# Attention steps reordered on every engine of a cross-attention and mixture-of-experts kernel, with TensorE's steps written out

## The chip, the cores and the metric

The kernel runs on one core of a Trainium2 chip. The metric is device time in microseconds of one execution. An engine issues its own instructions in program order, and engines meet only at semaphores. PE is TensorE, DVE is VectorE, ACT is ScalarE, POOL is GpSimd, and SP issues most of the DMAs.

## The reference

The input is 4 x 512 rows of 512 numbers. One layer of cross-attention (8 heads of 64 channels) and one mixture-of-experts layer with a shared expert follow each other, both with a residual.

```python
def _L0_xattn_ref(q, k, v, gamma):
    qk = jnp.einsum('bhdq,bhdl->bhql', qh, kh) * scale
    sm = jax.nn.softmax(qk, axis=-1)
    ret = jnp.einsum('bhql,bhdl->bhdq', sm, vh)
    return gamma * ret.reshape(B, Dv, Lq)
def _L0_ffn_ref(hidden_states, router_w, w_gate, w_up, w_down, sw_gate, sw_up, sw_down, shared_gate_w):
    shared = jnp.einsum('ts,sh->th', jax.nn.silu(x @ sw_gate) * (x @ sw_up), sw_down)
    ...
    routed = jnp.einsum('eth,te->th', expert_out, combine)
    shared_out = jax.nn.sigmoid(x @ shared_gate_w)[:, None] * shared
    return (routed + shared_out).reshape(B, S, Hd)
x = x + _L0_xattn_ref(_layernorm(x), ctx_2048, ctx_2048, L0_xattn_gamma)
x = x + _L0_ffn_ref(_layernorm(x), ...)
```

Queries are the normalised `x`; keys and values are both the context. Heads run over the channel rows, so 128 rows of `x` hold two heads.

## The kernel before

The kernel has three stages on the time axis: attention (to about 260 us), the shared expert (lines with `wsp`), and the routed experts. Only the first stage and what it hands over are touched. Every fp32 product is made of a rounded high half and the low rest (`qh`, `ql`, `kh`, `kl`, `pth`, `ptl` and so on).

Attention works on NT = 16 tiles of 128 rows, which is two heads each. For a tile `t` the work is, with the letters that the text uses:

- SP: `load_x` and `load_values` bring `xb` and `cn`; `store_rows`, `store_normed` and `store_columns` write the results.
- DVE `first_norm`, `aggregate(0)`, `variance(0)`, then POOL `inverse_deviation(0)`, `shift(0)`, `queries`, `queries_hi`, `queries_lo`, `keys_hi`, `keys_lo`: the operands of the scores.
- S0 to S3 (`scores`): six matmuls each on PE, into one of two double PSUM tiles. After each, DVE takes the maximum (`maxima`, L919) and ACT two exponentials (`exps`, L677). S(c+2) reuses the PSUM tile of S(c).
- T0 to T7 (`probs_T`, L1226): four transposes each on PE into one of the three PSUM banks `bT`, by the table `P_BANK`. ACT copies the high half (`probs_hi`, L683), DVE takes the rest (`probs_lo`, L929), and only then is the bank free. T0 to T3 want the exponentials of the first head, of which S3's is last.
- V0 to V7 (`times_v`, L1240 and L1242): two matmuls each into `bO`. After V3 and V7 ACT copies one half of the result (`low_half`, L696) and DVE adds (`halves`, L936), which frees `bO`.
- Val (`values_T`, L1254), Inv (`inverses`, L1248), Row (`rows_T`, L1260) and Log (`logits`, L1266) on PE: context transpose, softmax divisors (spread by POOL's `spread`), transposed rows of the result, and router logits.
- POOL `scaled`, `residual`, then DVE `second_norm`, `aggregate(1)`, `variance(1)`, then POOL `inverse_deviation(1)`, `shift(1)`, `rows_normed`: the rows `x2n` that Row transposes.

A step `i` mixes parts of tiles `i-4` to `i+4`. Each engine has its own list in a function `step(i)`, and that list is the only thing that sets the order. On PE step `i` of before holds T4 to T7 and V2 to V7 of tile i-1, S3 and T0 to T3 of tile i, and S0 to S2 of tile i+1. On PE steps 4 to 13 are five turns of a hardware loop with two steps in each turn, and waits whose values come from registers; all other steps and all other engines are written out.

In steps 9 to 12 POOL's list ends with `first_tokens`, which splits 128 tokens of the shared expert's first block (L568, L571). In step 16 ACT and DVE split the first two chunks of the shared expert's weights (`weights_hi`, `weights_lo`, 128 x 1536). PE begins the shared expert with `gate_up(0, 0)` and `gate_up(0, 1)`, which stand between the last attention steps; its first `down` is at L1366.

At the start SP's list runs `load_x(0)`, `load_values(0)`, `load_x(1)`, `load_values(1)`, `load_x(2)`, `small_ones()`, `load_x(3)`. The last line of `small_ones` writes `slot_rows` from `meta`: 39 KB in 4992 pieces of 8 bytes.

## Time and profile before

| | us |
|---|---|
| median of 3 runs | 898.32 (897.53 to 900.61) |
| profiled execution | 897.0 |
| its span | 895.2 |
| PE busy in the span | 850.4 |
| DVE, ACT, POOL busy | 568.3, 504.7, 438.6 |

The profile is of one execution: it has a span, and 1.8 us lie around it. Its busy times are of all three stages together. For the first stage the engines must be read window by window: the whole span has PE at 95%, but DVE at 63% only because the two later stages leave it idle, and the page's 40 slices show DVE at nine tenths through most of the first ten.

### The profile page before, as it was taken

How to read it: one execution, taken by the hardware profiler on the slowest of the kernel's cores; microseconds unless marked ns; L12 is line 12 of the kernel's file. 1: busy time of each engine (PE TensorE's matmuls, PEld its weight loads, DVE VectorE, ACT ScalarE, POOL GpSimd, SP SyncE). 2: the span in 40 equal slices, each digit the busy share in tenths (PEclk: the TensorE clock that was granted, in tenths of full speed). 3: DMA queues.
4: the chain of work that ended last, by engine and by line, in shares of the span. 5: the costliest groups of instructions: out<-in, count | busy, mean ns of one | idle time of the engine just before them, and what ended most of it. 6: DMA issues, size and time to landing. Idle time of an engine off the chain costs nothing.

```text
span 895.2 us, 13754 instructions
## 1 busy us (share of the span) xinstructions
PE 850.4 (95%) x4624; PEld 709.4 (79%) x4624; DVE 568.3 (63%) x819; ACT 504.7 (56%) x862; POOL 438.6 (49%) x422
## 2 busy tenths in 40 slices
PE   4999999999869999999999999999999999999993
PEld 2677777777658888888888888888899999999992
DVE  4999999999625533421312121125899999999991
ACT  4999999889543321121112111114888888888881
POOL 6576777875500000043320000002799999999983
PEclk9999999999979999999999999999999999999996
DMA  9113232241343313000310015444844444344342
GB/s 119 61 72 107 94 140 98 81 152 60 118 141 106 106 48 128 13 2 2 122 23 24 1 69 184 158 168 164 257 78 88 72 81 83 70 84 81 71 71 35
DMA packets 63236, 81.24 MB, mean 91 GB/s; under 512 B 15369, under 2 KB 34825, under 8 KB 63186
## 3 DMA queue, kind: packets, MB, share of 16 engines
q1 hardware_dynamic: 53426, 60.14, 22.0%
q0 software_dynamic: 9760, 20.49, 12.7%
q8 instruction: 25, 0.41, 0.2%
q14 instruction: 25, 0.20, 0.1%
HBM read 53.01 MB, written 27.60 MB: 90 GB/s over the span
## 4 chain that ended last, share of the span: by engine, by line
PE 86%; POOL 5%; DVE 3%; issue 2%; ACT 2%; DMA 2%; POOLq 0%; SPq 0%; DVEq 0%; ACTq 0%
PE scores L1352 9%; PE scores L1353 9%; PE scores L1354 9%; PE bank L1226 5%; PE scores L1217 5%; PE bank L1366 5%; PE bank L1367 5%; PE bank L1368 5%; PE bank L1453 3%; PE bank L1454 3%; PE bank L1452 3%; PE bank L1240 3%; PE scores L1428 3%; PE scores L1430 3%; PE scores L1429 3%; PE bank L1428 3%
## 5 line engine op out<-in xcount | busy, mean ns | idle before, releaser
L1009 DVE TENSOR_TENSOR sg<-scores,sg 128x512 f32<-128x512 f32 x44 | 30.4, 692 | 216.0 <-PE scores L1354 201.8
L1352 PE MATMUL scores<-x_hl,wsp 128*128 128x512 f32 x352 | 137.1, 389 | 0.0
L1354 PE MATMUL scores<-x_hl,wsp 128*128 128x512 f32 x352 | 137.0, 389 | 0.0
L1353 PE MATMUL scores<-x_hl,wsp 128*128 128x512 f32 x352 | 137.0, 389 | 0.0
L608 POOL DMA_INDIRECT slot_rows<-msrc,posi x32 | 33.4, 1045 | 185.4 <-PE scores L1354 178.9
L623 POOL DMA_INDIRECT xg<-x_normed_rows,meta x39 | 40.1, 1029 | 160.5 <-PE scores L1376 141.8
L782 ACT ACTIVATE sg<-scores 128x512 f32<-128x512 f32 x44 | 26.3, 598 | 159.7 <-PE scores L1354 159.7
L677 ACT ACTIVATE pb<-scores,negmax 128x512 f32<-128x512 f32 x128 | 88.1, 695 | 12.2 <-DVE negmax L919 12.2
L789 ACT ACTIVATE hh<-sg 128x512 fp32r<-128x512 f32 x44 | 27.8, 631 | 115.9 <-DVE sg L1009 100.9
L929 DVE TENSOR_TENSOR ptl<-bank,pth 128x512 fp32r<-128x512 f32 x128 | 87.1, 683 | 6.1 <-ACT pth L683 5.6
L919 DVE TENSOR_REDUCE negmax<-scores 128x2 f32<-128x1024 f32 x64 | 77.8, 1215 | 9.3 <-PE scores L1217 8.7
L683 ACT ACTIVATE pth<-bank 128x512 fp32r<-128x512 f32 x128 | 76.7, 600 | 12.1 <-PE bank L1226 10.9
L644 POOL TENSOR_TENSOR wd<-wex,wd 96x512 fp32r<-96x512 f32 x39 | 80.5, 2065 | 3.3
L1226 PE MATMUL bank<-ident,pb 128*128 128x128 f32 x512 | 78.6, 276 | 1.6 <-DVE ptl L929 1.5
L1226 PEld LDWEIGHTS bank<-ident,pb 128*128 128x128 f32 x512 | 60.1, 140 | 25.1 <-issue 9.8
L1366 PE MATMUL bank<-wsp,hh 128*128 128x512 f32 x176 | 69.8, 396 | 7.8 <-DVE hl L1011 7.2
L1352 PEld LDWEIGHTS scores<-x_hl,wsp 128*128 128x128 f32 x352 | 66.2, 188 | 13.8
L1353 PEld LDWEIGHTS scores<-x_hl,wsp 128*128 128x128 f32 x352 | 66.1, 188 | 13.7
L1354 PEld LDWEIGHTS scores<-x_hl,wsp 128*128 128x128 f32 x352 | 66.1, 188 | 13.7
L1125 DVE TENSOR_TENSOR wg<-wex,wg 128x1408 fp32r<-128x1408 f32 x39 | 63.4, 1627 | 12.5 <-ACT wg L808 12.5
L634 POOL DMA_INDIRECT out<-y,meta x39 | 63.7, 1634 | 13.0 <-issue 5.8
L1367 PE MATMUL bank<-wsp,hh 128*128 128x512 f32 x176 | 69.4, 394 | 0.0
(175 smaller groups left out, 2224.4 us busy)
## 6 DMA issues: line engine op xcount, KB each, us to landing
wex<-in_L_ffn_w_gate SPq DMA_DIRECT2D x8, 704.0 KB, 4.5
wex<-in_L_ffn_w_up SPq DMA_DIRECT2D x8, 704.0 KB, 5.9
xb<-in_x SPq DMA_DIRECT2D x16, 256.0 KB, 2.8
cn<-in_ctx SPq DMA_DIRECT2D x16, 256.0 KB, 2.7
x_rows<-xb SPq DMA_DIRECT2D x16, 256.0 KB, 2.0
x_normed_rows<-x2n SPq DMA_DIRECT2D x16, 256.0 KB, 2.0
x_normed_transposed<-x2T SPq DMA_DIRECT2D x16, 256.0 KB, 2.0
x_hl<-x_normed_transposed SPq DMA_DIRECT2D x4, 1024.0 KB, 5.2
```

The costliest lines, as they stand in the source:

```text
L634: g.indirect_dma_start(out=out, out_offset=bass.IndirectOffsetOnAxis(ap=meta[:, s, 0:1], axis=0), in_=y3[s % 2][:, :], in_offset=None, com ...
L644: gp.tensor_tensor(wd3[0:IR, 1, c], wex[0:IR, e, 2 * W3 + (IC - 1) * H:EW], wd3[0:IR, 0, c].bitcast(F32), ALU.subtract).then_inc(g_wd, 1)
L677: sc.activation(pb[t % 2][s][:, c, :], bSS[c % 2][:, s, :], ACT.Exp, bias=negmax[:, c, s:s + 1], scale=1.0, accum_out=rsum[:, c, s:s + 1]) ...
L683: sc.activation(pth[n % 4][:, :], bT[P_BANK[n]][:, :], ACT.Copy).then_inc(a_pth, 1)
L919: ve.tensor_reduce(negmax[:, c, :], bSS[c % 2][:, :, :], AX_X, ALU.max, negate=True).then_inc(d_max, 1)
L929: ve.tensor_tensor(ptl[n % 4][:, :], bT[P_BANK[n]][:, :], pth[n % 4][:, :].bitcast(F32), ALU.subtract).then_inc(d_ptl, 1)
L1226: ins = te.transpose(bT[P_BANK[n]][:, q * P:(q + 1) * P], pb[par][s][:, q, c * P:(c + 1) * P], ident[:, :])
L1352: te.matmul(bk[:, :], hi, xhi, start=(h == 0), stop=False)
L1353: te.matmul(bk[:, :], hi, xlo, start=False, stop=False)
L1354: ins = te.matmul(bk[:, :], lo, xhi, start=False, stop=(h == HC - 1))
L1366: te.matmul(bY[tt][:, :], th, hi, start=(c == 0), stop=False)
L1367: te.matmul(bY[tt][:, :], th, lo, start=False, stop=False)
```

## The change

Each engine's `step(i)` gets another list; the functions called are the same, apart from the PSUM bank of Inv and Row (from `bT[1]` to `bT[2]`) and the table `P_BANK`. Steps now run from -2 to 19 instead of -4 to 18. PE's loop is gone: its steps are all written out. PE's step `i` now holds T3 to T7 and all V of tile i-1, S2, S3 and T0 to T2 of tile i, and S0 and S1 of tile i+1. POOL does `queries`, `queries_hi`, `queries_lo` and `keys_hi` of tile i+2 in step i, and `keys_lo` a step later. `scaled` and `residual` of a tile come one step later; `first_tokens` moves to steps 10 to 13.

```diff
-        P_BANK = (0, 1, 0, 2, 0, 2, 0, 2)
+        P_BANK = (1, 0, 1, 0, 2, 0, 1, 0)
...
-            for i in range(-4, NT + 3):
+            for i in range(-2, NT + 4):
                 step(i)
...
             def step(i):
+                if there(i - 4):
+                    store_rows(i - 4)
+                    store_columns(i - 4)
+                if there(i + 2):
+                    load_x(i + 2)
+                    load_values(i + 2)
                 if there(i - 3):
                     store_normed(i - 3)
-                if there(i + 2):
-                    load_values(i + 2)
-                if there(i - 3):
-                    store_columns(i - 3)
-                if there(i + 4):
-                    load_x(i + 4)
-                if there(i - 1):
-                    store_rows(i - 1)
...
             load_values(1)
-            load_x(2)
             small_ones()
-            load_x(3)
-            for i in range(NT + 3):
+            for i in range(NT + 4):
                 step(i)
...
+                if there(i - 3):
+                    shift(1, i - 3)
+                if there(i - 2):
+                    scaled(i - 2)
                 if there(i - 3):
                     rows_normed(i - 3)
+                if there(i - 2):
+                    residual(i - 2)
                 if there(i + 1):
-                    queries_lo(i + 1)
                     keys_lo(i + 1)
+                if there(i + 2):
+                    inverse_deviation(0, i + 2)
+                    shift(0, i + 2)
+                    keys_hi(i + 2)
+                    queries(i + 2)
+                if there(i):
+                    spread(i)
+                if there(i + 2):
+                    queries_hi(i + 2)
                 if there(i - 2):
                     inverse_deviation(1, i - 2)
...
+                if there(i + 2):
+                    queries_lo(i + 2)
+                if 10 <= i < 10 + TB:
+                    first_tokens(i - 10)
...
-            for i in range(-4, 4):
-                step(i, i // 2, i % 2)
-            with pe.Fori(2, NI - 1) as half:
-                for par in range(2):
-                    step(2 * half + par, half, par)
-            for i in range(NT - 2, NT + 1):
+            for i in range(-2, NT + 1):
                 step(i, i // 2, i % 2)
             gate_up(0, 0, 0)
             step(NT + 1, (NT + 1) // 2, (NT + 1) % 2)
             gate_up(0, 1, 0)
-            for i in range(NT + 2, NT + 3):
+            for i in range(NT + 2, NT + 4):
                 step(i, i // 2, i % 2)
```

First place: SP's queue at the very start, from the third tile's load in before to the first load of the steps. Before:

```order
L339 DMA xb2_83<-in_x 128x512
L377 DMA gam_53<-in_L0_xattn_gamma 128x1
L378 DMA rg_80<-in_L0_ffn_router_w 8x512
L379 DMA rg_80<-in_L0_ffn_shared_gate_w 1x512
L381 DMA out<-zrow_112 128x512
L382 DMA x2_normed_rows<-zrow_112 128x512
L384 DMA slot_rows<-meta_60 128x39x2
L339 DMA xb3_84<-in_x 128x512
L344 DMA cn0_69<-in_ctx_2048 128x512
```

After:

```order
L377 DMA gam_53<-in_L0_xattn_gamma 128x1
L378 DMA rg_80<-in_L0_ffn_router_w 8x512
L379 DMA rg_80<-in_L0_ffn_shared_gate_w 1x512
L381 DMA out<-zrow_112 128x512
L382 DMA x2_normed_rows<-zrow_112 128x512
L384 DMA slot_rows<-meta_60 128x39x2
L339 DMA xb2_83<-in_x 128x512
L344 DMA cn0_69<-in_ctx_2048 128x512
```

The load of tile 2 (`xb2`) moved from ahead of the small transfers to behind `slot_rows`, into the place that tile 3's load had.

Second place: DVE's queue at the start, from the maximum of S0 of tile 0. `BN_STATS` on `xb2` is `first_norm(2)`. Before:

```order
L919 TENSOR_REDUCE negmax_66<-scores0 128x2
L892 BN_STATS stats_61<-xb2_83 128x6
L919 TENSOR_REDUCE negmax_66<-scores1 128x2
L940 COPY rgT_52<-bank4 128x36
L913 TENSOR_TENSOR vs0_89<-bank6,vs0_89 128x4x128
L919 TENSOR_REDUCE negmax_66<-scores0 128x2
L919 TENSOR_REDUCE negmax_66<-scores1 128x2
```

After:

```order
L915 TENSOR_REDUCE negmax_66<-scores0 128x2
L915 TENSOR_REDUCE negmax_66<-scores1 128x2
L915 TENSOR_REDUCE negmax_66<-scores0 128x2
L888 BN_STATS stats_61<-xb2_83 128x6
L936 COPY rgT_52<-bank4 128x36
L909 TENSOR_TENSOR vs0_89<-bank6,vs0_89 128x4x128
L915 TENSOR_REDUCE negmax_66<-scores1 128x2
```

`first_norm(2)` moved from behind the first maximum to between the third and the fourth; the fourth maximum now stands behind it.

Third place: PE in step 3, around S3 of tile 3 (`scores1`) and Row of tile 0 (`x2n0`). Before:

```order
L1248 MATMUL bank6<-ident_49,rspr_106 128x128 x4
L1240 MATMUL bank4<-pth3_98,vs0_89 128x512
L1242 MATMUL bank4<-ptl3_102,vs0_89 128x512
L1226 MATMUL bank7<-ident_49,pb01_92 128x128 x4
L1217 MATMUL scores1<-kh1_72,qh1_76 128x512 x2
L1217 MATMUL scores1<-kl1_74,qh1_76 128x512 x2
L1217 MATMUL scores1<-kh1_72,ql1_78 128x512 x2
L1226 MATMUL bank5<-ident_49,pb01_92 128x128 x4
L1260 MATMUL bank6<-ident_49,x2n0_108 128x128 x4
L1240 MATMUL bank4<-pth0_95,vs0_89 128x512
L1242 MATMUL bank4<-ptl0_99,vs0_89 128x512
L1226 MATMUL bank7<-ident_49,pb01_92 128x128 x4
```

After:

```order
L1237 MATMUL bank4<-pth2_97,vs0_89 128x512
L1239 MATMUL bank4<-ptl2_101,vs0_89 128x512
L1214 MATMUL scores1<-kh1_72,qh1_76 128x512 x2
L1214 MATMUL scores1<-kl1_74,qh1_76 128x512 x2
L1214 MATMUL scores1<-kh1_72,ql1_78 128x512 x2
L1237 MATMUL bank4<-pth3_98,vs0_89 128x512
L1239 MATMUL bank4<-ptl3_102,vs0_89 128x512
L1223 MATMUL bank6<-ident_49,pb01_92 128x128 x4
L1257 MATMUL bank7<-ident_49,x2n0_108 128x128 x4
L1223 MATMUL bank5<-ident_49,pb01_92 128x128 x4
L1214 MATMUL scores0<-kh0_71,qh0_75 128x512 x2
L1214 MATMUL scores0<-kl0_73,qh0_75 128x512 x2
```

V3 moved from ahead of S3 to behind it, T5 to ahead of it, and T7 and S0 of the next tile now follow Row directly, with V4 and V5 behind.

## Rows read from the trace of the kernel before

**Rows 1.** Busy time by engine, clock and DMA share in one step's window each.
```profile
core 0: us, PE busy (x) PEld busy (x) DVE busy (x) ACT busy (x) POOL busy (x), PEclk, DMA share, GB/s
80.25:93.87 13.62, 13.62 (x94) 10.25 (x92) 13.08 (x23) 12.75 (x31) 9.83 (x14) 1.00 0.29 97
...
148.34:162.62 14.28, 13.71 (x94) 10.25 (x93) 13.14 (x23) 12.75 (x31) 11.64 (x16) 1.00 0.27 93
...
205.47:219.09 13.62, 13.62 (x94) 10.24 (x93) 12.53 (x20) 12.74 (x31) 7.92 (x9) 1.00 0.18 68
```
**Rows 2.** Timeline of PE inside step 6: start, duration, instruction.
```profile
94.78 0.60 PE L1226 MATMUL bank<-ident,pb 128*128 128x128 f32 x4
95.31 0.50 PE L1217 MATMUL scores<-kh,qh 64*128 64x512 f32 x2
...
96.20 0.66 PE L1226 MATMUL bank<-ident,pb 128*128 128x128 f32 x4
96.69 0.60 PE L1260 MATMUL bank<-ident,x2n 128*128 128x128 f32 x4
97.05 0.49 PE L1240 MATMUL bank<-pth,vs 128*128 128x512 f32 x1
...
97.60 0.60 PE L1226 MATMUL bank<-ident,pb 128*128 128x128 f32 x4
97.96 0.48 PE L1240 MATMUL bank<-pth,vs 128*128 128x512 f32 x1
...
98.60 0.50 PE L1217 MATMUL scores<-kh,qh 64*128 64x512 f32 x2
...
101.40 0.96 PE L1266 MATMUL bank<-rgT,x2T 128*128 128x9 f32 x8
102.29 0.50 PE L1217 MATMUL scores<-kh,qh 64*128 64x512 f32 x2
```
**Rows 3.** Timeline of ACT in the same step.
```profile
95.22 0.60 ACT L696 ACTIVATE lob<-bank 64x512 f32<-64x512 f32 x1
...
98.24 0.60 ACT L683 ACTIVATE pth<-bank 128x512 fp32r<-128x512 f32 x1
98.73 0.68 ACT L677 ACTIVATE pb<-scores,negmax 128x512 f32<-128x512 f32 x1
...
99.39 0.60 ACT L702 ACTIVATE x2T<-bank 128x512 f32<-128x512 f32 x1
99.87 0.70 ACT L677 ACTIVATE pb<-scores,negmax 128x512 f32<-128x512 f32 x1
```
**Rows 4.** SP's DMA queue at the start, timeline.
```profile
5.19 0.49 SPq L384 DMA_DIRECT2D slot_rows<-meta  x1
5.72 8.50 SPq L339 DMA_DIRECT2D xb<-in_x  x1
```
**Rows 5.** The tile view of `xb` from 4 to 9 us, which holds that one load.
```profile
DMA to landing us min/median/max: 15.4/15.4/15.4
```
**Rows 6.** Timeline of DVE and of PE: the fourth maximum, and S2 of two tiles.
```profile
17.75 1.23 DVE L919 TENSOR_REDUCE negmax<-scores 128x2 f32<-128x1024 f32 x1 [0.57 <-PE scores L1217]
...
23.99 0.50 PE L1217 MATMUL scores<-kh,qh 64*128 64x512 f32 x2
...
50.65 0.50 PE L1217 MATMUL scores<-kh,qh 64*128 64x512 f32 x2
```
**Rows 7.** The chain that ended last, a piece in step 9.
```profile
146.43 0.56 POOL x_hl L568
...
148.35 0.76 POOL xn L517
```
**Rows 8.** Timeline of PE at the end of attention.
```profile
220.51 0.50 PE L1217 MATMUL scores<-kh,qh 64*128 64x512 f32 x2
...
238.79 0.48 PE L1352 MATMUL scores<-x_hl,wsp 128*128 128x512 f32 x1
...
261.83 0.76 PE L1366 MATMUL bank<-wsp,hh 128*128 128x512 f32 x1 [7.24 <-DVE hl L1011]
```

More of the change, by code:

```diff
@@ L740, in step @@
                 if there(i - 1):
-                    probs_hi(i - 1, 7)
-                if there(i):
-                    exps(i, 3, 0)
+                    low_half(i - 1, 0)
+                    probs_hi(i - 1, 6)
                 if there(i - 3):
@@ L746, in step @@
                 if there(i):
+                    exps(i, 3, 0)
+                if there(i - 1):
+                    probs_hi(i - 1, 7)
+                if there(i):
                     exps(i, 3, 1)
                     probs_hi(i, 0)
-                if there(i - 1):
-                    low_half(i - 1, 1)
-                if there(i):
                     probs_hi(i, 1)
@@ L760, in step @@
                     probs_hi(i, 2)
-                if there(i + 1):
-                    values_hi(i + 1)
+                if there(i - 1):
+                    low_half(i - 1, 1)
+                if there(i - 3):
+                    logits(i - 3)
             over_tiles(step)
@@ L952, in step @@
             def step(i):
-                if there(i + 2):
-                    first_norm(i + 2)
+                if there(i - 1):
+                    probs_lo(i - 1, 1)
                 if there(i):
@@ L958, in step @@
                     probs_lo(i - 1, 2)
-                if i == 0:
-                    router_columns()
-                if there(i):
-                    values_lo(i)
+                if there(i - 2):
+                    halves(i - 2, 1)
                 if there(i - 1):
@@ L968, in step @@
                     maxima(i, 2)
+                if there(i + 2):
+                    first_norm(i + 2)
                 if there(i - 1):
                     probs_lo(i - 1, 4)
-                if there(i - 2):
-                    second_norm(i - 2)
+                if i == 0:
+                    router_columns()
+                if there(i):
+                    values_lo(i)
                 if there(i - 1):
-                    halves(i - 1, 0)
                     probs_lo(i - 1, 5)
@@ L980, in step @@
                 if there(i - 1):
+                    halves(i - 1, 0)
                     probs_lo(i - 1, 6)
                 if there(i - 2):
-                    aggregate(1, i - 2)
+                    second_norm(i - 2)
                 if there(i + 2):
@@ L987, in step @@
                     probs_lo(i - 1, 7)
-                if there(i - 2):
-                    variance(1, i - 2)
                 if there(i + 2):
```

117 lines of the change are left out of this document (50 added, 67 removed).

## Prediction

> **What bounds the kernel now.** I read the whole-span page first, then the busy time window by window, then the timelines of one step. In one ordinary attention step [rows 1] PE is busy 13.62 of 13.62 us, DVE 13.08, ACT 12.75, POOL 9.83, at full clock. So PE sets the pace, and DVE is 0.5 us behind it: a step cannot get much shorter, and an order that makes either wait shows at once. The second window of [rows 1] is one of four of that kind: 14.28 us, with POOL at 11.64. There POOL's `first_tokens` takes 1.92 us (146.43 to 148.35) on the chain that ended last [rows 7], and S0 of the next tile waits for its keys. Start and end of the stage are chains of waits [rows 4 to 6, 8]. After 261.83 [rows 8] the change touches nothing, so it is a shift of that moment that I forecast. Everything is summed against the profiled execution, 897.0 us with a span of 895.2; it lies 1.3 us under the median of 898.32.
>
> **1. Written out instead of a loop: 0.** PE's window inside the loop (first of [rows 1]) and that of written-out steps (third) both last 13.62 us, PE full in both. The register waits and the branch cost nothing that PE's queue doesn't hide. The Trainium skill (Runtime: NRT & Kernel Launch, Instruction fetch mechanics) says that a taken branch breaks the sequential prefetch of instructions and that kernels prefer full unrolling. By that rule the five turns would each have given something back; PE's idle time in the loop window is under 0.1 us, so it is at most 0.1 x 5 = 0.5 us here, and I take none. The trace doesn't bear the rule out here.
>
> **2. The start: +3.0.** This is the largest term. `slot_rows` is written in 4992 pieces, and the load issued right behind it holds SP for 8.50 us [rows 4] and lands 15.4 us after its issue [rows 5], at 5.72 + 15.4 = 21.1. Before, that is tile 3, which DVE wants only a step later, so it costs nothing. Now it is tile 2. One load fewer stands ahead, so it is issued about 0.5 us earlier: I take 20.6 for the landing; 19.6 if the 256 KB that no longer precede it make way wholly, 21.1 if nothing changes. DVE's queue has `first_norm(2)` ahead of the fourth maximum of tile 0. So behind 20.6 come the statistics, the small copy and `values_lo`, about 1.4 us, and the maximum of S3 starts at 22.0, where it now starts at 17.75 [rows 6]. Behind DVE wait ACT's exponentials of S3, T0 and all else. Part is made up. From the fourth maximum to S2 of tile 1 the trace has 23.99 - 17.75 = 6.24 us [rows 6]; in the new order S0 of tile 1 is done by then, and what is left is one maximum (1.23), two exponentials, two copies, two exponentials, which by [rows 3] (0.66 and 0.49 each) is 1.23 + 1.32 + 0.98 + 1.32 + some 0.15 = 5.0. S2 of tile 1 starts at 27.0 instead of 23.99: +3.0, with 2.0 and 3.5 for the other landings. Had the tile been there in time, the same walk puts the fourth maximum at 18.5 and S2 at 23.5: -0.5.
>
> **3. Two early steps: -1.3.** From S2 of tile 1 to S2 of tile 3 the trace takes 50.65 - 23.99 = 26.66, that is 13.33 each [rows 6], although Row and Log are not there yet. PE's own work in them is 13.62 less Row 0.36 and Log 0.89 [rows 2], about 12.4; the rest is waiting. In the new order T's copies stand further ahead of V, and I find no wait in the first above 0.2 us: 12.5. In the second DVE has nearly its full list, 12.53 being its load where `first_norm` and its two small followers are missing (third window of [rows 1]): 12.85. Gain 0.8 + 0.5. Bounds: 0.3, if DVE's order costs what it costs now, and 1.7, if both are at PE's 12.4.
>
> **4. Twelve full steps: +0.5.** PE's groups are the same; only neighbours change [rows 2]. T costs 0.36 (97.60 to 97.96), 0.53 ahead of S, and 0.49 behind S (96.20 to 96.69); V costs 0.55, and 0.64 ahead of S (97.96 to 98.60); S is 0.89. Before, S is entered once from a T and thrice from V or Log, and left twice into a T; now it is entered twice from T and twice from V, and left once into a transpose: +0.08 - 0.13 = -0.05, so PE's own length is 13.57. Against it stands a new loop of waits. S3, V3, T6, Row, T7, S0, V4, T0 is PE's order, and T0 needs the first exponential of S3. ACT's list before that has `low_half` (after V3), `probs_hi` 6 and `rows_T`. From V3's start: 0.64 as from a transpose to its copy (97.60 [rows 2] to 98.24 [rows 3]), 0.2 for the second matmul, 0.62 `low_half`, 0.49, 0.48 (99.39 to 99.87), and 0.9 for the exponential with its sum until PE may go: 3.35. PE's own way from V3 to T0 is 0.55 + 0.36 + 0.36 + 0.53 + 0.89 + 0.55 = 3.24. So T0 waits 0.1 in each step and the step is 13.66, 0.04 over now: 12 x 0.04 = +0.5. If ACT is 0.1 faster than that, 13.55 and -0.9; if T1's bank (freed by the DVE copy of T7, which I find 0.1 us ahead of need) is late by 0.1 more, 13.77 and +1.8. The other edges that I walked (score tiles, banks, `bO`, the four `pth` buffers) have 0.3 us or more to spare.
>
> **5. The four stretched steps: -0.5.** They now cost 14.28 - 13.62 = 0.66 each [rows 1], 2.7 in all. In the new order POOL's list from DVE's `variance(0)` to the end of `keys_lo` is one whole step of POOL, 9.83 busy and some 0.3 of gaps, plus 1.92 for `first_tokens`: 12.05. Adding up PE's list by the costs of term 4, T7 starts 6.5 and S0 7.06 into a step. T7's copy on ACT comes behind the exponential, at 8.4, and DVE's rest of it (0.6) and `variance(0)` end at 9.75. S0 of the next tile is wanted at 13.66 + 7.06 = 20.7; keys come at 9.75 + 10.15 = 19.9 without `first_tokens` and at 21.8 with it. That is 1.1 late. But the wait stands behind T7, so it also moves the next step's need by 1.1 and not its `variance(0)`; of four such steps only every second waits: 2 x 1.1 = 2.2. Bounds: none of it (-2.7), or all four (+1.7).
>
> **6. The end: +1.2.** From S3 of tile 15 to the first matmul of the shared expert the trace takes 238.79 - 220.51 = 18.3 [rows 8]; without scores on PE, DVE is what all wait for, with two weight chunks of 128 x 1536 among its list. The new order leaves two more operations behind the last maximum (`halves` of tile 14, `second_norm` of 13, 0.6 each), and one gap less than 0.2 us goes. Then Log of tile 13 shares a bank with Inv of tile 15 and must wait for ACT's copy of it, 0.4. I make it 19.5: +1.2, bounds 0 and +1.8. Behind it both `gate_up` blocks, Row and Log of tiles 14 and 15, and the wait of 7.24 us for the next weight chunk, which SP issues only after the last tile's columns, stand as before.
>
> **Sum.** 3.0 - 1.3 + 0.5 - 0.5 + 1.2 = +2.9: 899.9 for a profiled execution like this one, and 898.3 + 2.9 = 901.2 on the median. What a measurement of this kernel can tell from no change is about 0.3%, 2.7 us, so 901.0 is the line, and the forecast lies at it.
>
> **Rivals.**
> A. The load of tile 2 is in time, or DVE isn't held. For it: before, ahead of the small transfers, it never made DVE wait. Against it: [rows 4, 5]. The start is then -0.5: 901.2 - 3.5 = 897.7, no change that can be measured. 15%.
> B. Faster, by one mechanism: transposes run further ahead of their use, so that neither ACT nor POOL is ever waited for. It decides if POOL's keys come 1 us earlier than I find and T0 doesn't wait. Terms 3 to 5 are then -1.7, -0.9 and -2.7, together -5.3 where I have -1.3. With my start that is 897.2; with a landing at 19.6 and no loss at the end 895.0, under 895.6 and so faster. 10%, of which most needs A too.
> C. Slower: a step with so little to spare falls into a longer cycle, say T1 or V4 late by 0.2 more in each of twelve steps, since DVE's 13.08 of 13.66 leaves 0.6 and its list waits in order. +2.4: 903.6. It decides from 0.1 us of lateness per step. 20%.
> D. The loop is what mattered: -0.5 at most by term 1, 900.7. 4%.
>
> **Chances.** My forecast with its bounds has 51%, and lies a little more than half above 901.0: 29% slower, 22% same. A adds 14 to same, C 20 to slower, D 4 to same, B 8 to faster and 2 to same, A 1 to faster. Slower 0.49, same 0.42, faster 0.09. The range, 897.4 to 904.4, leaves out B's better half at the low end and a C that adds to my upper bounds at the high end, and takes in A.
>
> **What would show it.** Right: in the changed profile DVE idles for some 3.5 us before the statistics at L888, released by a DMA of `xb`, near 20.6; S2 of tile 1 near 27; full steps of 13.6 to 13.7 us from Inv to Inv; two steps near 14.7; `gate_up` 19.5 us behind the last S3; the wait for `hl` near 7.2 us again. Wrong: tile 2's load landing before 17 us, PE waiting on ACT or DVE for more than 0.2 us in every full step, a step under 13.5, or a new gap anywhere after `gate_up(0, 0)`.

## The result and the profile after

The changed kernel takes 908.82 us (median of 5 executions, 903.85 to 909.85) against 899.62 (897.53 to 901.42) for the kernel before on the same chip: ratio 1.0096, 95% interval 1.0074 to 1.0119. It is slower, as forecast with the largest chance, but by 9.2 us instead of 2.9, and outside the range. The profiled execution of after is the shortest of its five, 903.85 with a span of 902.1; the other four take 906.84 to 909.85. The page of after, line of busy times by engine, to set beside the table of before:

```profile
PE 854.4 (95%) x4624; PEld 710.8 (79%) x4624; DVE 568.9 (63%) x819; ACT 501.9 (56%) x862; POOL 441.1 (49%) x422
```

The work is the same; PE is busy 4.0 us longer and idle for the other 2.9. There are two questions: the 6.9 us between the two profiled executions (902.1 - 895.2), and the further 3 to 6 us of the others.

**The start.** Timeline of DVE, then of PE, after (start, duration, what the engine idled for):

```profile
16.60 1.23 DVE L915 TENSOR_REDUCE negmax<-scores 128x2 f32<-128x1024 f32 x1 [1.97 <-PE scores L1214]
21.07 0.69 DVE L888 BATCH_NORM_STATS2 stats<-xb 128x6 f32<-128x512 f32 x1 [3.24 <-DMA xb<-in_x]
...
22.37 1.21 DVE L915 TENSOR_REDUCE negmax<-scores 128x2 f32<-128x1024 f32 x1
```
```profile
24.54 1.94 PE L1223 MATMUL bank<-ident,pb 128*128 128x128 f32 x8 [2.68 <-ACT pb L673]
26.41 0.79 PE L1214 MATMUL scores<-kh,qh 64*128 64x512 f32 x2
27.00 0.63 PE L1214 MATMUL scores<-kl,qh 64*128 64x512 f32 x2
...
27.99 1.50 PE L1223 MATMUL bank<-ident,pb 128*128 128x128 f32 x8
29.41 0.50 PE L1214 MATMUL scores<-kh,qh 64*128 64x512 f32 x2
29.75 0.40 PE L1214 MATMUL scores<-kl,qh 64*128 64x512 f32 x2
```

The wait for tile 2 is the one forecast. The fourth maximum is at 22.37, where [rows 6] has 17.75. But S2 of tile 1 comes at 29.41, not at 27.0. The PE rows say why: up to 28 us PE runs at its lower level (1.2 GHz), 0.63 for a multiplication that takes 0.40 at 29.75, and 1.94 for eight transposes. From 24.54 to 29.41 PE issues eight transposes, S1 of tile 1 and eight transposes. At the costs of the higher level (0.43 and 0.53 for a group of four, 0.89 for S) that is 2.8 us instead of 4.9. So about 2 us of it is the level; this is an estimate, since no run has the late load and the higher level throughout.

**The middle.** Windows of after, one full step and one with `first_tokens`, to set beside [rows 1] and with its columns; behind them the timeline of PE inside a full step, to set beside [rows 2]:

```profile
105.82:119.51 13.69, 13.69 (x94) 10.18 (x93) 13.08 (x25) 12.49 (x31) 9.81 (x13) 1.00 0.31 99
...
158.00:172.40 14.40, 14.00 (x95) 10.25 (x93) 13.79 (x24) 13.20 (x33) 11.45 (x15) 1.00 0.25 93
```
```profile
115.74 0.60 PE L1223 MATMUL bank<-ident,pb 128*128 128x128 f32 x4
116.18 0.60 PE L1257 MATMUL bank<-ident,x2n 128*128 128x128 f32 x4
116.61 0.60 PE L1223 MATMUL bank<-ident,pb 128*128 128x128 f32 x4
117.14 0.50 PE L1214 MATMUL scores<-kh,qh 64*128 64x512 f32 x2
...
118.61 0.60 PE L1223 MATMUL bank<-ident,pb 128*128 128x128 f32 x4
118.96 0.48 PE L1237 MATMUL bank<-pth,vs 128*128 128x512 f32 x1
```

A full step is 13.69 instead of 13.62, and PE waits nowhere in it. What differs is what a group of transposes costs: 0.44 and 0.43 where transposes follow (115.74 to 116.18 to 116.61), 0.35 where a multiplication by `vs` follows (118.61 to 118.96). The trace of before has such a pair too, Val ahead of T, at the same price of 0.43 (PE, before):

```profile
103.68 0.60 PE L1254 MATMUL bank<-ident,cn 128*128 128x128 f32 x4
104.11 0.60 PE L1226 MATMUL bank<-ident,pb 128*128 128x128 f32 x4
```

In after, Inv and Row have come to stand ahead of a T; each costs 0.43 there instead of 0.35 to 0.36. Two of the four stretched steps are left, at 14.4, as in this row:

```profile
172.63 0.50 PE L1214 MATMUL scores<-kh,qh 64*128 64x512 f32 x2 [0.63 <-issue]
```

**The end.** Timelines of PE and of DVE, after, against [rows 8]:

```profile
225.30 0.50 PE L1214 MATMUL scores<-kh,qh 64*128 64x512 f32 x2
...
242.13 0.50 PE L1237 MATMUL bank<-pth,vs 128*128 128x512 f32 x1 [2.08 <-DVE att L932]
...
245.45 0.48 PE L1350 MATMUL scores<-x_hl,wsp 128*128 128x512 f32 x1
...
268.53 0.77 PE L1364 MATMUL bank<-wsp,hh 128*128 128x512 f32 x1 [7.30 <-DVE hl L1008]
```
```profile
239.26 2.22 DVE L940 TENSOR_TENSOR wsp<-stg,wsp 128x1536 fp32r<-128x1536 f32 x1
241.40 0.67 DVE L932 TENSOR_TENSOR att<-bank,lob 64x512 f32<-64x512 f32 x1
```

V4 of the last tile waits 2.08 us for `bO`, since `halves` now stands behind the second weight chunk on DVE. From the last S3 to the shared expert: 20.15 us instead of 18.28. Before, PE wasn't full here either, but waited in two shorter pieces (PE, before):

```profile
232.94 0.66 PE L1226 MATMUL bank<-ident,pb 128*128 128x128 f32 x4 [1.27 <-DVE ptl L929]
...
236.98 0.50 PE L1242 MATMUL bank<-ptl,vs 128*128 128x512 f32 x1 [0.91 <-DVE ptl L929]
```

The 6.9 us of the profiled pair, place by place:

| | before | after | difference | forecast |
|---|---|---|---|---|
| S2 of tile 1 starts | 23.99 | 29.41 | +5.42 | +3.0 |
| S2 of tile 1 to S3 of tile 15 | 196.52 | 195.89 | -0.63 | -1.3 |
| S3 of tile 15 to `gate_up(0, 0)` | 18.28 | 20.15 | +1.87 | +1.2 |
| to the first `down` | 23.04 | 23.08 | +0.04 | 0 |
| to the end of the span | 633.37 | 633.57 | +0.20 | 0 |

### The profile page after: what moved, and what is told of

Read it like the earlier page. It is cut to its first block, busy times and chain, and to the rows that moved or that the text cites. A ratio compares the mean times of both kernels' runs of the same rounds, so it can differ in the third digit from the quotient of the medians.

```text
span 902.1 us, 13623 instructions
## 1 busy us (share of the span) xinstructions
PE 854.4 (95%) x4624; PEld 710.8 (79%) x4624; DVE 568.9 (63%) x819; ACT 501.9 (56%) x862; POOL 441.1 (49%) x422
## 4 chain that ended last, share of the span: by engine, by line
PE 90%; DMA 3%; DVE 2%; ACT 2%; issue 1%; SPq 1%; POOL 0%; POOLq 0%; DVEq 0%; ACTq 0%
PE scores L1350 9%; PE scores L1352 9%; PE scores L1351 9%; PE bank L1223 6%; PE scores L1214 5%; PE bank L1364 5%; PE bank L1366 5%; PE bank L1365 5%; PE bank L1237 4%; PE bank L1239 3%; PE bank L1445 3%; PE bank L1446 3%; PE bank L1447 3%; PE scores L1421 3%; PE scores L1423 3%; PE scores L1422 3%
## 5 line engine op out<-in xcount | busy, mean ns | idle before, releaser
L925 DVE TENSOR_TENSOR ptl<-bank,pth 128x512 fp32r<-128x512 f32 x128 | 86.4, 683 | 13.0 <-ACT pth L679 12.5
L1364 PE MATMUL bank<-wsp,hh 128*128 128x512 f32 x176 | 69.8, 397 | 7.9 <-DVE hl L1008 7.3
L1223 PEld LDWEIGHTS bank<-ident,pb 128*128 128x128 f32 x512 | 63.2, 144 | 15.8 <-issue 3.4
L630 POOL DMA_INDIRECT out<-y,meta x39 | 67.2, 1723 | 12.6 <-issue 5.7
L1366 PE MATMUL bank<-wsp,hl 128*128 128x512 f32 x176 | 69.5, 395 | 0.0
```

The source lines that it names most:

```text
L630: g.indirect_dma_start(out=out, out_offset=bass.IndirectOffsetOnAxis(ap=meta[:, s, 0:1], axis=0), in_=y3[s % 2][:, :], in_offset=None, com ...
L925: ve.tensor_tensor(ptl[n % 4][:, :], bT[P_BANK[n]][:, :], pth[n % 4][:, :].bitcast(F32), ALU.subtract).then_inc(d_ptl, 1)
L1223: ins = te.transpose(bT[P_BANK[n]][:, q * P:(q + 1) * P], pb[par][s][:, q, c * P:(c + 1) * P], ident[:, :])
L1364: te.matmul(bY[tt][:, :], th, hi, start=(c == 0), stop=False)
L1366: ins = te.matmul(bY[tt][:, :], tl, hi, start=False, stop=(c == SC - 1))
```

## Experiments on the start

**e1: tile 2's load back ahead of the small transfers, all else as after.**

```diff
                 if there(i + 2):
-                    load_x(i + 2)
+                    if i > 0:
+                        load_x(i + 2)
...
             load_values(1)
+            load_x(2)
             small_ones()
```

> The changed kernel with one part undone: tile 2 is loaded ahead of the small transfers again, as before the change. Theory 1 (the late load is most of the loss: in the changed profile DVE waits 3.2 us for it, and PE then runs its next matmuls at the low clock level, 0.80 us for one that otherwise takes 0.50): S2 of tile 1 starts at 23.4 to 24.2 instead of 29.4, everything behind shifts by as much, and the profiled execution is at 898 to 899 instead of 903.85. Rival 1 (the new order starts slower whatever the load does): S2 of tile 1 not before 26.5 and a time above 901. If the timed runs of the changed kernel lie 3 to 6 us above its profiled one because the wait at the start differs between executions, the spread goes away here; if the spread stays, it comes from the hand-over to the shared expert.

Measured 900.34 us (896.19 to 903.21, 10 executions), 1.0022 times before (1.0003 to 1.0041): 4.2 us under the same changed kernel measured beside it (e4 below, 904.56), 5.8 under the median of all its executions (906.1, below). DVE doesn't wait, but S2 of tile 1 starts at 26.80. Timeline of DVE, then of PE, e1:

```profile
17.52 0.68 DVE L890 BATCH_NORM_STATS2 stats<-xb 128x6 f32<-128x512 f32 x1
...
19.52 1.23 DVE L917 TENSOR_REDUCE negmax<-scores 128x2 f32<-128x1024 f32 x1 [0.29 <-PE scores L1216]
```
```profile
21.71 1.94 PE L1225 MATMUL bank<-ident,pb 128*128 128x128 f32 x8
...
25.15 1.72 PE L1225 MATMUL bank<-ident,pb 128*128 128x128 f32 x8
26.80 0.51 PE L1216 MATMUL scores<-kh,qh 64*128 64x512 f32 x2
```

The load was the cause of the wait and of most of the time. The start that I had forecast for a load in time, 23.5, is missed by 3.3 us, and again the 1.94 is there: PE's lower level is a second cost, which is there with the load in time too.

**e2: the kernel before with tile 2's load moved behind `slot_rows`.** One line moved in SP's list:

```diff
             load_values(1)
-            load_x(2)
             small_ones()
+            load_x(2)
             load_x(3)
```

> The kernel before with one part of the change alone: tile 2's load put behind the small transfers, behind the slot_rows write. Its DVE list has first_norm(2) behind the first maximum already, so DVE is held even earlier, from 13.2 to about 20.6. Theory 1: S2 of tile 1 comes 6 to 9 us later than 23.99 and the time is 903 to 907. Rival 1: under 900.5, since the load alone costs little.

Measured 905.06 (903.67 to 906.61, 4 executions), 1.0071 (1.0054 to 1.0088). This one line makes the old order slower by 6.6 us. DVE, e2:

```profile
19.94 0.69 DVE L892 BATCH_NORM_STATS2 stats<-xb 128x6 f32<-128x512 f32 x1 [6.79 <-DMA xb<-in_x]
```

S2 of tile 1 starts at 31.92, against 25.77 in e3, which has the old order too and a start at the lower level. So most of the damage of the change needs no reordering of steps at all.

**e5: e1, and 48 transposes of the identity on PE right after the constants are there.**

```diff
             pe.wait_ge(g_const, N_CONST)
+            for _ in range(48):
+                te.transpose(bT[2][:, 0:P], ident[:, :], ident[:, :])
```

> The kernel with tile 2 loaded early (e1) and, in addition, 48 transposes of the identity on PE into an unused bank between the constants and the first scores, so that PE isn't idle for its first 10 us. In e1 S2 of tile 1 started at 26.8 and PE's scores took 0.80 us each up to 24, against 0.50 behind that. Theory 2 (the new order leaves PE with gaps of 1.2 to 1.5 us at the start, in which it stays at the low clock level; that, and not a missing result, is the rest of the loss at the start): the scores of tile 0 take 0.50 us, S2 of tile 1 starts at 23.4 to 24.4, and the time is 2.4 to 3.4 us under e1's. Rival 2 (the start is bound by DVE and ACT, whose durations don't depend on PE's clock): S2 of tile 1 after 25.8 and the time within 1 us of e1's.

PE, e5:

```profile
10.24 0.49 PE L1216 MATMUL scores<-kh,qh 64*128 64x512 f32 x2 [0.43 <-POOL kl L536]
...
24.10 0.50 PE L1216 MATMUL scores<-kh,qh 64*128 64x512 f32 x2
```

The first scores take 0.49 instead of 0.79, and S2 of tile 1 starts at 24.10 instead of 26.80. So the level costs at least 2.7 us at the start; in e5 too it falls once, with 0.79 for the scores at 21.50. Yet the time is 900.72 (899.04 to 901.61, 7 executions), 1.003 (1.0019 to 1.0042), the same as e1. In the trace 1.5 us of the gain are lost again between the last S3 and `gate_up` (21.67 us against 20.15 in e1) and 1.6 from there to the first `down`, by the clock. Windows of e5, PE alone:

```profile
core 0: us, PE busy (x), PEclk, DMA share, GB/s
...
238.00:243.00 5.00, 5.00 (x19) 0.51 0.00 0
243.00:248.00 5.00, 5.00 (x19) 0.81 0.27 105
```

**e8: after, with `slot_rows` written in 39 pieces of 1 KB.** The loads keep the order of after; the numbers are laid out in another tile, so that each piece is whole. SP also waits for this write before it loads the first weight chunk.

```diff
+        minit = place("minit", [SLOTS, P, 2], I32)
...
-                sp.dma_start(meta_d.rearrange("(s p) c -> p s c", p=P), meta[:, :, :]).then_inc(st_meta0, 16)
+                sp.dma_start(meta_d.rearrange("(s p) c -> s p c", p=P), minit[:, :, :]).then_inc(st_meta0, 16)
```

> The changed kernel with tile 2's load where the change put it, but the slot_rows write ahead of it made of 39 pieces of 1 KB instead of 4992 of 8 bytes (the same values, from another tile). Theory 1 (it is that write that holds the load 15 us): tile 2 lands before 12 us, SP's issue of it takes 0.4 to 0.5 us instead of 6.9, DVE doesn't wait for it, and the start and the time equal e1's: S2 of tile 1 at 26.8 if PE is at the low level, 24 if not; 4 to 6 us under the changed kernel. Rival (it is the queue as such, or the two writes of zeros): landing after 15 us and the time within 2 us of the changed kernel's.

SP's queue, e8:

```profile
4.72 0.40 SPq L386 DMA_DIRECT2D slot_rows<-minit  x1
5.16 0.90 SPq L341 DMA_DIRECT2D xb<-in_x  x1
```

In after the same load takes SP 6.94 us and lands 15.9 us after its issue; here it is 0.90 and 4.2. DVE doesn't wait, S2 of tile 1 starts at 26.77, and the time is 900.94 (899.24 to 902.62, 10 executions), 1.0021 (1.0006 to 1.0036): e1 again, by another way. It is the 4992 small pieces, and not the place in the queue as such, that hold up tile 2.

## Experiments on the middle

**e3: the kernel before, PE's loop written out.** Steps -4 to 16 come from one Python loop.

> The kernel before with PE's loop of five turns written out, and nothing else. My theory: nothing, within 0.5 us of the kernel before, and a step of 13.62 us in what was the loop. Rival (the written-out program itself costs, by more instruction loading): over 2 us slower, with idle time of PE that no semaphore explains; or, the other way, 0.5 us or more faster by the branches saved.

Measured 898.03 (896.17 to 899.24, 10 executions), 0.9989 (0.998 to 0.9999). Full steps last 13.61 to 13.62 as before. The four stretched steps last 14.14 instead of 14.28, with this wait in place of one of 0.57:

```profile
155.32 0.50 PE L1217 MATMUL scores<-kh,qh 64*128 64x512 f32 x2 [0.43 <-POOL kl L538]
```

So the loop costs nothing where PE doesn't wait, and some 0.14 us each time it really waits. The longer wait is there in all four stretched steps, 0.57 to 0.59 against 0.43 to 0.46, although the loop branches only after every second step. That a wait on a register's value is seen later is my reading; no run tests it.

**c4: the kernel before with T7 ahead of V4,** so that Row's transposes are followed by T7's.

```diff
                 if there(i - 1):
-                    times_v(i - 1, 1 - par, 4)
                     freed((d_ptl, 8, i - 1, 5), (d_ptl, 8, i - 1, 3), (a_lg, 1, i - 4, 0), (d_ptl, 8, i - 2, 7))
                     probs_T(i - 1, 1 - par, 7)
+                    times_v(i - 1, 1 - par, 4)
                     times_v(i - 1, 1 - par, 5)
```

> The kernel before with one exchange in TensorE's steps: T7 ahead of V4, so that the rows' transposes are followed by T7's, a group of transposes behind another. Theory (a group of transposes takes 0.43 to 0.44 us when transposes follow and 0.35 to 0.36 when a multiplication does): each full step 13.70 instead of 13.62, +0.08, over twelve such steps about +1 us: 899 to 900 us against 898.5. Rival (the position of a group costs nothing, the 0.07 of the changed kernel's step is elsewhere): steps of 13.62. If T7's DVE copy is not ready, a wait shows in front of T7 and the run says nothing on either.

Full steps last 13.74. PE, c4:

```profile
113.11 0.60 PE L1260 MATMUL bank<-ident,x2n 128*128 128x128 f32 x4
113.63 0.66 PE L1226 MATMUL bank<-ident,pb 128*128 128x128 f32 x4
114.04 0.48 PE L1240 MATMUL bank<-pth,vs 128*128 128x512 f32 x1
```

Row takes 0.52 where [rows 2] has 0.36. The direction is the theory's, the size is not: +0.12 per step instead of +0.08. I had 0.43 for such a place; the other 0.09, with the 0.66 of T7, looks like a short wait for T7's operands or bank that no row names. T7 itself takes 0.41 instead of 0.36, and V5 ahead of the scores 0.55 instead of 0.64: 0.16 + 0.05 - 0.09 = 0.12. So the exchange moves three prices at once and doesn't isolate one; the pure price is the 0.43 of Val ahead of T, which both kernels have. The time is 899.23 (896.98 to 901.17, 10 executions), 1.0004 (0.9993 to 1.0014), from -0.6 to +1.3 us: 1.4 us over twelve steps would lie at its edge. The step lengths in the trace carry this, not the time.

**e7: after, with `first_tokens(i)` a step later and behind `keys_lo` on POOL.**

```diff
                 if there(i + 1):
                     keys_lo(i + 1)
+                if 11 <= i < 11 + TB:
+                    first_tokens(i - 11)
...
-                if 10 <= i < 10 + TB:
-                    first_tokens(i - 10)
```

> The changed kernel with first_tokens moved within POOL's list from its end to behind keys_lo of the next step, where POOL waits for DVE's variance anyway. Theory 4 (my loop of two steps: only every second of the four steps waits, 0.6 to 0.7 us each in the changed profile, since POOL's list from the variance to the keys is late by that): both waits of S0 (172.6 and 200.7) go, all full steps take 13.69, and the time is 1.2 to 1.4 us lower. Rival: POOL is full in these steps, and the wait moves to the queries of the tile after: no change or slower.

(The expectation of c1 below says DVE for this edit; it is POOL's list.) Windows of e7, an ordinary step and one with `first_tokens`:

```profile
158.00:171.70 13.70, 13.70 (x93) 10.19 (x93) 13.07 (x23) 12.49 (x30) 9.78 (x14) 1.00 0.28 98
171.70:185.40 13.70, 13.70 (x93) 10.16 (x93) 13.08 (x23) 12.49 (x30) 11.61 (x16) 1.00 0.26 86
```

POOL's 11.6 us fit in a step if the keys go first. The time of 904.5 (901.15 to 905.93, 6 executions), 1.0063 (1.0043 to 1.0084), lies in the spread of after and can't show 1.3 us; the step lengths do. The pair f4 and c1 below points the same way.

## Experiments on the end, and on the spread

**e6: after, with the second weight chunk behind the copies of T7 on ACT and DVE.** The same two moves, one on each engine; DVE's shown:

```diff
-                if i == NT:
-                    weights_lo(1)
...
+                if i == NT:
+                    weights_lo(1)
```

> The changed kernel with one edit at the end: ACT and DVE split the second weight chunk behind their copies of T7 of the last tile, not between T5 and T6. In the changed profile PE waits 2.08 us for halves in front of V4 of tile 15, behind that split. Theory 3 (the end is bound by DVE's queue, and the splits are what holds PE): the wait in front of V4 goes under 0.5 us, gate_up(0, 0) starts 1.6 to 2.2 us earlier relative to S3 of tile 15 (20.15 in the changed profile), and so does all behind it: median 2 us under the changed kernel's. In addition, if the long wait is what sometimes brings the clock down in gate_up(0, 0) (0.72 in one profile), the spread upward shrinks. Rival 3: gate_up(0, 1) or the first down then waits for the second chunk and gives it back: same time.

The wait ahead of V4 is gone and S3 to `gate_up` takes 18.29 us, the 18.28 of before. Time 901.25 (900.08 to 904.05, 6 executions), 1.0035 (1.0017 to 1.0052). That is 4.9 under the 906.1 of all executions of the changed kernel, more than the 1.9 us of the row.

**e4: the changed kernel again,** beside e1 to e3.

> The changed kernel again, unaltered, for a second profile and more executions: its timed runs were 903.85 to 909.85. If the spread is of the start, S2 of tile 1 or the landing of tile 2 differs from the first profile (29.41 and 21.1) by as much as the time does. If it is of the clock at the hand-over, the start is the same and the first down matmuls and the gate_up behind them run at the low level for longer, 1.2 us more for each 2.4 us of low clock; the mean granted clock of the execution is then under 0.98.

904.56 (903.75 to 908.27, 4 executions), 1.008 (1.0056 to 1.0103). Its profiled execution, 903.75, has S3 to `gate_up` at 21.60 instead of 20.15, with a granted clock of 0.72 in 243 to 248 us. That brought the clock behind V4's wait under suspicion.

**c3: after, with 7 and 22 transposes of the identity on PE ahead of V0 and V4 of the last tile,** into a bank that is free there. The 7 stand behind a wait for the last exponentials. The diff shows the 22 only.

```diff
                 if there(i + 1):
                     scores(i + 1, 1 - par, 0)
+                if i == NT:
+                    for _ in range(22):
+                        te.transpose(bank[0][:, 0:P], ident[:, :], ident[:, :])
```

> The changed kernel with 7 and 22 extra transposes of the identity on PE ahead of V0 and V4 of the last tile, where PE waits 0.7 and 2.1 us; bank 0 is free then, nothing reads them. Theory (the wait ahead of V4 is what PE's clock falls after): gate_up(0,0) and the multiplications behind it run at 0.50 us per 128x512 in every execution, S3(15) to gate_up(0,0) is at most 20.3, and the median is 1 to 2 us under the changed kernel's 904.5 to 909, with less spread between runs. Rival (the wait itself is all that is lost): the same 904.5 to 909 us with the same spread.

PE, c3:

```profile
240.71 2.57 PE L1313 MATMUL scores<-ident 128*128 128x128 f32 x22
243.03 0.48 PE L1237 MATMUL bank<-pth,vs 128*128 128x512 f32 x1
```

S3 to `gate_up` took 20.22 at a granted clock of 1.00. The time is 904.51 (902.06 to 905.09, 4 executions), 1.0056 (1.004 to 1.0073). None is over 905.1, while nine of the fourteen executions of after that I have are. The median, though, is that of e4, and not 1 to 2 us under it as expected; the start of this execution is 0.8 us later than in after. The narrower spread agrees with the theory; with four executions it is no proof.

**f1, f2, f3, f5, f6: the changed kernel five more times,** one execution with a trace each, to catch a long one.

> The changed kernel, for one more trace. Theory (a lower clock, not a longer wait, makes the executions of 905 to 910 us): if this execution is over 906 us, its mean granted clock is under 0.981 and one window between 225 and 300 us, or one behind 590 us, shows a granted clock under that of the trace of 903.85 us, long enough for the difference; the waits at the start and ahead of V4 are as before. Rival (x2's load lands later): DVE's wait for xb is over 6 us and the first down multiplication lies 4 us or more behind 268.5 for that reason alone.

> As f1: over 906 us only with a mean granted clock under 0.981 and a stretch at the lower clock that the trace of 903.85 us does not have, by the theory; with a longer wait for x2's load by the rival.

> As f1: over 906 us only with a mean granted clock under 0.981 and a stretch at the lower clock that the trace of 903.85 us does not have, by the theory; with a longer wait for x2's load by the rival.

> The changed kernel once more. Theory from f1 to f3: an execution over 906 us shows more time at a granted clock under 1.00 in 238 to 253 us and in 262 to 285 us than f3 (0.50 in 243 to 248, 0.50 in 270 to 275, 0.88 in 275 to 280), or a further such stretch behind; one of 900 to 904 us shows less. Rival: a longer one shows the same clocks as f3 and a longer wait at the start or behind 600 us.

> The changed kernel once more, as the run beside it: by the theory over 906 us only with more time at a granted clock under 1.00 between 238 and 285 us than f3, and 900 to 904 us with less; by the rival the same clocks as f3 and a longer wait elsewhere.

They took 900.31, 903.88, 905.29, 908.88 and 906.85 us, nearly the whole spread. Windows of f1 (900.31), then of f5 (908.88), PE alone:

```profile
238.00:243.00 5.00, 2.92 (x17) 1.00 0.41 157
243.00:248.00 5.00, 5.00 (x27) 1.00 0.02 3
248.00:253.00 5.00, 4.22 (x25) 1.00 0.42 161
```
```profile
238.00:243.00 5.00, 2.55 (x16) 0.90 0.41 157
243.00:248.00 5.00, 5.00 (x18) 0.50 0.01 3
248.00:253.00 5.00, 5.00 (x16) 0.58 0.27 105
```

And the first matmul behind the wait ahead of V4, in f1 and in f5:

```profile
241.35 0.50 PE L1237 MATMUL bank<-pth,vs 128*128 128x512 f32 x1 [2.07 <-DVE att L932]
```
```profile
242.63 0.79 PE L1237 MATMUL bank<-pth,vs 128*128 128x512 f32 x1 [2.08 <-DVE att L932]
```

The wait is the same to 0.01 us; the level behind it is not. In the whole set:

| changed kernel | us | S2 of tile 1 | S3 to `gate_up` | clock 238-243, 243-248, 248-253 | first `down` | rest of span |
|---|---|---|---|---|---|---|
| f1 | 900.31 | 28.68 | 20.16 | 1.00, 1.00, 1.00 | 267.25 | 631.2 |
| after | 903.85 | 29.41 | 20.15 | 1.00, 1.00, 1.00 | 268.53 | 633.6 |
| f2 | 903.88 | 28.03 | 21.47 | 0.75, 0.91, 1.00 | 268.68 | 633.4 |
| f3 | 905.29 | 28.16 | 21.74 | 0.91, 0.50, 0.91 | 270.30 | 633.2 |
| f6 | 906.85 | 28.01 | 22.83 | 0.71, 0.50, 0.77 | 271.98 | 633.1 |
| f5 | 908.88 | 30.00 | 22.81 | 0.90, 0.50, 0.58 | 273.36 | 633.7 |

From after to f5 the span grows by 5.0: 0.6 at the start, -0.1 in the middle, 2.66 in S3 to `gate_up`, 1.66 from there to `down`, 0.2 in the rest. So 4.3 of the 5.0 us lie behind that wait, where f5 has the lower level and after doesn't. This bears the theory out; its rival it doesn't, since DVE's wait for tile 2 is 4.17 in f5 and 3.24 in after, and the start gives 0.6. f1's shorter rest has another place of the same kind: the low level that follows the wait for the next chunk is over soon after 270 us in f1 (0.98 in 270 to 275) and lasts nearly to 275 in after (0.54). e1 is like f1 there (1.00 in 270 to 275, 632.1 for the rest), e8 is not (633.6).

**f4: after with the edits of e6 and e8; c1: with those of e6, e7 and e8.**

> The changed kernel with slot_rows in whole pieces and chunk 1's weights later, without the edit of first_tokens. By the rows the two places add up (2.6 at the start, 1.9 ahead of gate_up(0,0)): S2(1) near 26.8 or 25, S3(15) to gate_up(0,0) 18.2 to 18.3, and 1.3 over c1 for the stretched steps: 897.5 to 898.5 us. If each edit alone had removed one and the same stretch at a lower clock, the two together stay at 900 to 901 us.

> The changed kernel with three edits at once: slot_rows written in 39 whole pieces, first_tokens(i) put behind the next step's keys_lo on DVE (so that no step of the middle is stretched), and weights_hi/lo(1) put behind the copies of T7 in the tail. If the three places found so far (x2's landing, the stretched steps, the wait ahead of V4) are separate terms that add up: S2(1) near 26.8, every step of the middle at 13.70, S3(15) to gate_up(0,0) 18.3, first down multiplication near 263 us, and a time of 896 to 899 us. If the clock's dips, and not these places, make the time, the median stays at 900 to 902 us, as it did with each of the three edits alone.

f4: 898.18 (896.51 to 898.79, 10 executions), 0.9994 (0.998 to 1.0007). c1: 896.55 (894.88 to 898.51, 10 executions), 0.9982 (0.9972 to 0.9992). Both are where expected. c1 has every full step at 13.68 to 13.71, S3 to `gate_up` at 18.22, and S2 of tile 1 at 24.95, the start being in part at the higher level. The edit of `first_tokens` is 1.6 us between the two medians, 1.1 by their ratios to before (they ran on different chips, and the intervals overlap); by the steps it is 1.3 (165.1 us for the twelve steps from S2 of tile 3 in e7, 166.4 in after). With these three repairs the new order is as fast as the old is without them.

**c2: the kernel before, written out, with the three edits.**

> The kernel before, written out, with the same three edits: slot_rows in whole pieces, first_tokens behind the next step's keys_lo, chunk 1's weights behind the copies of T7. If the old order's cheaper steps (13.62 instead of 13.70) and the three places add up: S2(1) at 24 to 26, every step at 13.62, S3(15) to gate_up(0,0) 16.4 to 17.5, first down multiplication near 259 us, and a time of 893 to 896 us, under both kernels. If the order of the change is itself worth something at the start or the end, this is no faster than the changed kernel with the same edits (896 to 899 us).

895.77 (893.57 to 897.94, 9 executions), 0.9969 (0.9956 to 0.9983): faster than both kernels, and 0.8 us under c1, which ran beside it. So with the same three edits in both, the new order brings nothing; whether it costs those 0.8 us the intervals don't tell. A `first_tokens` step of c2:

```profile
158.00:171.62 13.62, 13.62 (x95) 10.23 (x94) 13.04 (x23) 12.73 (x31) 11.66 (x16) 1.00 0.31 99
```

One part missed: S3 to `gate_up` stayed at 18.40, where 16.4 to 17.5 was expected. The later chunk brings nothing in the old order, where `halves` stands ahead of it already: PE's second wait falls from 0.91 to 0.23, but Log then waits 0.72 for ACT's copy of the rows. Against e3 the gain is 2.3 us by the medians and 1.8 by the ratios, and the stretched steps alone account for 4 x 0.52 = 2.1.

## Why the prediction was wrong, step by step

The step that failed throughout is PE's clock. The sum priced every PE row at its higher level and had no term for what a wait does to the level: at the start that is some 2 of the 7.04 us that the forecast put at 5.0 (term 2), and behind the wait ahead of V4 it is 0 to 4.3 us that no term had. Terms 4 and 6 missed smaller parts for reasons of their own.

**Term 1, the loop: right within 0.6.** PE's full steps are the same in both forms, as [rows 1] said. I had missed that written-out waits end 0.14 us sooner where PE really waits; e3 puts the whole of it at 0.6 us by the steps. The rule of the Trainium skill (Runtime: NRT & Kernel Launch, Instruction fetch mechanics) that full unrolling is preferred has the right sign here. The trace gives no sign that the fetching of instructions is the reason: PE has no idle time at the branch in the full steps, and the 0.14 is there in all four stretched steps, of which only every second ends in a branch.

**Term 2, the start: right mechanism, wrong size.** Landing (21.1 for 20.6), DVE's wait (3.24 for 3.5) and the fourth maximum (22.37 for 22.0) came about as worked out. The step that failed is "what is left ... 5.0". It priced PE at its higher level, because the profile of before has S2(0) and all that follows at 0.50, and [rows 6] gave me its 23.99 as the base. Measured it is 7.04, of which PE at the lower level is about 2 by the estimate above. The old order starts at either level: e3 has S2 of tile 1 at 25.77 with the same list. I had read a start at the better level as the start, and asked nowhere what PE's own idle time would do to its clock.

**Term 3, the early steps: -0.3 instead of -1.3.** The two steps take 12.58 and 13.15 (12.5 and 12.85 forecast), a gain of 0.93. But the third, 14.32 from S2 to S2, gives 0.63 back: there the context transpose waits 0.20 for DVE, and V0 comes 0.78 behind it instead of 0.41. A gain of 0.3 is my own lower bound, DVE's order setting the pace until the pipeline is full.

**Term 4, full steps: +0.07 instead of +0.04, and for another reason.** The wait at T0 isn't there. PE's own list is 13.69, not 13.57. I priced a group of transposes by what stands behind it only for scores and multiplications, and let Row, Inv, Log and T follow each other at 0.36. The one such pair in [rows 2], T into Row at 96.20, took 0.49, and I put that down to the scores ahead of it alone. For a neighbour that I had not looked up, I took the cheapest price, though the trace of before has the pair, Val ahead of T at 103.68, at 0.43. Inv and Row, 0.07 more each, are the 0.12 between 13.57 and 13.69. c4 supports this in sign.

**Term 5, stretched steps: right mechanism, wait too long.** Two of four wait, by turns, as worked out; each by 0.7 instead of 1.1, so -1.2 instead of -0.5. In e7 and c2, where only POOL's order is changed for these steps, they are gone.

**Term 6, the end: +1.87 instead of +1.2 in the profiled execution.** What I named (two operations more on DVE, Log's bank) isn't what is late, and its parts add up to about 1.4 rather than the 1.2 that I took. `halves` stands behind the second weight chunk, 2.22 us, and V4 waits for it; e6 takes away that wait and with it the whole term.

**What no term had: the clock behind the new wait.** Eleven traces have the 2.1 us ahead of V4. In seven of them (f2, f3, f5, f6, e4, e5, e7) PE's level falls behind it, in four (after, f1, e1, e8) it doesn't. Where the wait is gone or filled (e6, f4, c1, c3) it doesn't fall there, nor in the old order (before, e3, c2, c4); e2, the old order with the late load, is an exception, with 0.93 and 0.73 between 243 and 253 us. Before has two waits there, of 1.27 and 0.91, and after one of 2.08 with smaller ones around it. Whether the length in one piece is what matters is not tested. This low level is what lifts the traced executions f3, f5 and f6 above its 903.85. All fourteen executions of the changed kernel have their median at 906.1 (measured at different times and on more than one chip); the first five happened to lie high.

The sum of the measured terms for the profiled pair, 5.4 - 0.6 + 1.9 + 0.2 = 6.9, leaves nothing over. Of the 7.6 us that the forecast missed, 4.0 are in that pair: the start 2.4, the middle 0.7, the end's wait 0.7, the rest 0.2. The other 3.6 are between the executions: the profiled one of after lies 5.0 under its median, that of before 1.3 under the one I added to, and f5 shows 4.3 us of low level for such a difference. The direction came from term 2, and e1 and e2 confirm it. Rival C came nearest with 903.6, but by a loss in each full step, and there PE waits nowhere. Rival A is refuted twice: the load was late, and with the load in time e1 is at 900.34, not at 897.7. Of rival B one condition came true, T0 doesn't wait, but the full steps are no shorter for it, and in two of the `first_tokens` steps PE still waits for POOL's keys, 0.6 us each. Rival D has the right sign, with 0.5 us in e3, and decides nothing.

**Open.** Why the level falls behind the same 2.08 us in one execution and not in the next, and why e1 and e8, whose traces keep the wait, gain 5 to 6 us against 906.1 where their start explains 2.6. Against the first trace of after, which is without that low level, e8's is 2.3 us shorter, which is its start, and e1's is 4.0 shorter: 2.6 at the start and 1.5 behind the first `down`, where the low level is over sooner. The rest would be executions with the low level, as after has many. The ranges of e1 and e8 reach from 896.2 to 903.2, so they may simply fall less often; their one trace each doesn't tell.

## What to carry to other kernels

When an order moves a transfer behind many small pieces, price the pieces: here 39 KB in 4992 pieces cost more than all the reordering of steps. When an edit gives PE a new long wait, count the wait and also the time behind it at the lower clock, and expect it in only some executions: here 2.1 us of waiting in one piece, and from 0 to 4.3 us more behind it. A single profiled execution may lie at the edge of the spread, so a start or a hand-over that ran at the better level is not yet the rule. And compare an order with the old one after the same repairs in both: c1 and c2 differ by 0.8 us, where after and before differ by 9.2.

## What the runs showed of the hardware

A load issued behind `slot_rows` in 8-byte pieces held SP's queue for 6.94 us and landed after 15.9 (after); behind the same number of bytes in 1 KB pieces 0.90 and 4.2 (e8). A group of four transposes ran in 0.35 to 0.36 us ahead of a 128x512 multiplication (0.41 with scores just before it) and in 0.43 to 0.44 ahead of other transposes (before and after). Behind one wait of 2.04 to 2.08 us the granted clock fell to as low as 0.50 for a window of 5 us in some traces of the same kernel (f3, f5, f6) and stayed at 1.00 in others (after, f1). PE kept busy with 48 useless transposes before 10 us had its first scores at 0.49 instead of 0.79, and lost what it had gained more than 210 us later (e5, one trace). Between 10 and 28 us the column of the granted clock shows 1.00 for after while multiplications take 0.63 and 0.66; so at the very start the durations must be read, not that column.
